# The last tile's mean from TensorE, and 640 columns of the third tile finished by ScalarE and GpSimd, in a role adapter with layernorm

## What is computed

```python
h = jnp.einsum('bsh,bhk->bsk', hidden_states, W_down[role]) + b_down[role][:, None, :]
h = jax.nn.gelu(h, approximate=False)
u = jnp.einsum('bsk,bkh->bsh', h, W_up[role]) + b_up[role][:, None, :]
y = hidden_states + u
mean = jnp.mean(y, axis=-1, keepdims=True)
var = jnp.mean(jnp.square(y - mean), axis=-1, keepdims=True)
yn = (y - mean) * jax.lax.rsqrt(var + LN_EPS)
return yn * gamma[role][:, None, :] + beta[role][:, None, :]
```

## Time and profile before

| | |
|---|---|
| median of 3 runs | 362.35 us (362.21 to 362.82) |
| profiled execution | 362.48 us |
| its span, first to last instruction | 360.7 us |
| TensorE busy | 353.2 us, 98% |
| VectorE busy | 285.6 us, 79% |
| ScalarE busy | 185.0 us, 51% |
| GpSimd busy | 59.8 us, 17% |
| DMA moved | 96.61 MB, mean 268 GB/s |
| granted TensorE clock, mean | 0.998 |

### The profile page before, as it was taken

How to read it: one execution, slowest core, us unless ns; L and a number is a source line. 1 busy time by engine, 2 the same in 40 slices (tenths; PEclk the granted TensorE clock), 3 DMA queues, 4 the chain that set the end, 5 groups by cost and what they waited for, 6 DMA issues and landing times.

```text
span 360.7 us, 4991 instructions
## 1 busy us (share of the span) xinstructions
PE 353.2 (98%) x1559; PEld 290.2 (80%) x1559; DVE 285.6 (79%) x301; ACT 185.0 (51%) x303; POOL 59.8 (17%) x75
## 2 busy tenths in 40 slices
PE   9999999999999999999999999999999999999992
PEld 4888888888888888888888888888888888888882
DVE  3788999298993989759996699957989489893886
ACT  4785556761368415682256814476234862255133
POOL 0000222003220213102140022300232003320003
PEclk9999999999999999999999999999999999999999
DMA  6999999962999549994699927999099981745023
GB/s 187 393 408 409 410 393 358 355 237 87 333 336 362 219 121 370 330 344 172 172 363 343 353 107 244 341 360 352 40 297 348 377 315 53 240 147 204 1 115 120
DMA packets 27804, 96.61 MB, mean 268 GB/s; under 512 B 3218, under 2 KB 3858, under 8 KB 27794
## 3 DMA queue, kind: packets, MB, share of 16 engines
q1 hardware_dynamic: 23186, 81.14, 62.8%
q10 hardware_dynamic: 4608, 15.34, 11.0%
HBM read 79.70 MB, written 16.78 MB: 267 GB/s over the span
## 4 chain that ended last, share of the span: by engine, by line
PE 92%; DVE 3%; ACT 2%; issue 1%; POOL 1%; POOLq 0%; DVEq 0%; ACTq 0%
PE down_ps L311 48%; PE up_ps L318 42%; DVE rows L683 1%; PE up_ps L432 1%; DVE rows L688 1%; ACT squares L488 1%; DVE rows L742 0%; POOL rstd L603 0%; DVE up_ps L720 0%; POOLq L44 0%; ACT h_full L478 0%; ACT h_hi L480 0%; ACT neg_mean_scaled L485 0%; POOL var_eps L601 0%; DVE down_ps L705 0%
## 5 line engine op out<-in xcount | busy, mean ns | idle before, releaser
L311 PE MATMUL down_ps<-x_hi,wd_hi 128*128 128x512 f32 x256 | 81.2, 390 | 0.1
L311 PE MATMUL down_ps<-x_lo,wd_hi 128*128 128x512 f32 x256 | 80.9, 389 | 0.0
L311 PE MATMUL down_ps<-x_hi,wd_lo 128*128 128x512 f32 x256 | 80.8, 389 | 0.0
L318 PE MATMUL up_ps<-wu_hi,h_hi 128*128 128x512 f32 x248 | 76.4, 389 | 0.0
L318 PE MATMUL up_ps<-wu_lo,h_hi 128*128 128x512 f32 x248 | 76.4, 389 | 0.0
L318 PE MATMUL up_ps<-wu_hi,h_lo 128*128 128x512 f32 x248 | 76.3, 389 | 0.0
L601 POOL TENSOR_TENSOR var_eps<-var,eps 128x1 f32<-128x1 f32 x31 | 22.7, 733 | 292.0 <-ACT squares L488 292.0
L485 ACT ACTIVATE neg_mean_scaled<-row_sum 128x1 f32<-128x1 f32 x31 | 6.3, 203 | 124.7 <-DVE rows L688 124.7
L676 DVE TENSOR_TENSOR h_lo<-h_full,h_hi 128x512 fp32r<-128x512 f32 x32 | 22.2, 693 | 46.6 <-ACT h_hi L480 46.6
L311 PEld LDWEIGHTS down_ps<-x_hi,wd_hi 128*128 128x128 f32 x256 | 47.9, 188 | 11.1 <-issue 0.9
L311 PEld LDWEIGHTS down_ps<-x_hi,wd_lo 128*128 128x128 f32 x256 | 48.0, 188 | 10.0
(11 more groups left out here) (64 smaller groups left out, 274.2 us busy)
## 6 DMA issues: line engine op xcount, KB each, us to landing
wu_stage<-W_up SPq DMA_DIRECT2D x32, 512.0 KB, 7.0
rows<-x SPq DMA_DIRECT2D x32, 512.0 KB, 7.4
x_stage<-xT SPq DMA_DIRECT2D x30, 512.0 KB, 7.1
wd_stage<-W_down SPq DMA_DIRECT2D x30, 512.0 KB, 8.6
out<-rows ACTq DMA_DIRECT2D x28, 512.0 KB, 4.6
b_up_row<-b_up SPq DMA_DIRECT2D x8, 512.0 KB, 5.1
gamma_row<-gamma SPq DMA_DIRECT2D x8, 512.0 KB, 9.5
beta_row<-beta SPq DMA_DIRECT2D x8, 512.0 KB, 10.3
```

What stands on the lines that cost most here:

```text
L311: return pe.matmul(down_ps[:, kc, :], wd_part[:, n, c * K + kc * P:c * K + (kc + 1) * P], x_part[:, n, c * S:(c + 1) * S], start=start, st ...
L318: mm = pe.matmul(up_ps[:, t % 2, half], h_part[:, kc, t * P:(t + 1) * P], wu_part[:, kc, half], start=(kc == 0 and h_part is h_hi and wu_p ...
```

## The change

Before the last tile's product is there, its mean can be known: the sum of a row of h·W_up is h times the row sums of W_up. In the last batch ScalarE sums the rows of the four parts of `wu_stage` (`sum_wu`, an Identity with an accumulator over 1024 columns, into `wu_sum`), the sums are split into hi and lo like W_up and placed in two further columns of `wu_hi` and `wu_lo`, whose rows become H + 2 wide for all batches (the second further column is zero). The product of the last tile starts with columns 768 to 1023 and these two (258 columns), so the row sum of the projection lies in PSUM after the first part. ScalarE sums the residual (`sum_last_residual`), and `last_mean` puts both together. The parts are then centred on the true mean at once, into `centred` in SBUF (`centre_part`), squared by ScalarE from there (`part_variance`), multiplied by gamma from `centred` into `rows` (`scale_part`), and finished (`finish_piece`); the shift and its three steps on GpSimd are gone.

The third tile is finished by VectorE for columns 0 to 383 only; ScalarE multiplies the other 640 by the inverse deviation (`scale_tile`) and GpSimd adds beta (`finish_tile_columns`). The third tile's store waits for both.

The diff, cut to its core:

```diff
+    THIRD_COLS = 3 * P
...
-        wu_hi = sb("wu_hi", [P, KC, H], F32R)
-        wu_lo = sb("wu_lo", [P, KC, H], F32R)
+        wu_hi = sb("wu_hi", [P, KC, H + 2], F32R)
+        wu_lo = sb("wu_lo", [P, KC, H + 2], F32R)
+        wu_sum = sb("wu_sum", [P, KC, 2], F32)
...
+        LAST_PARTS = (POOL_PIECE,) + PIECES
+        LAST_BANKS = (down_ps[:, 0, 0:POOL_COLS], last_tile[:, PIECES[0]], last_tile[:, PIECES[1]])
+        LAST_MOVING = (slice(H - POOL_COLS, H + 2),) + PIECES
+        LAST_OUT = (down_ps[:, 0, 0:POOL_COLS + 2],) + LAST_BANKS[1:]
+        PROJECTED_SUM = down_ps[:, 0, POOL_COLS:POOL_COLS + 1]
...
+            sp.wait_ge(pool_third_normed, 1)
+            store_last(NT - 2)
...
-                        for part, bank in zip(LAST_PARTS, LAST_BANKS):
+                        pe.wait_ge(wu_sum_split, 1)
+                        for part, bank in zip(LAST_MOVING, LAST_OUT):
...
+            def sum_wu(i):
...
+                act.activation(squares[:, :], wu_stage[:, i, :], ACT.Identity,
+                               accum_out=wu_sum[:, i, 0:1]).then_inc(wu_sum_ready, 1)
+
+            def sum_last_residual():
+                act.wait_ge(biased, NT * B)
+                act.wait_ge(var_ready, NT * (B - 1) + 2)
+                act.activation(squares[:, :], rows[:, NT - 1, :], ACT.Identity,
+                               accum_out=residual_sum[:, :]).then_inc(residual_sum_ready, 1)
+
+            def part_variance(i):
...
+                act.wait_ge(last_part_centred, i + 1)
+                act.activation(squares[:, LAST_PARTS[i]], centred[:, (NT - 1) % 2, LAST_PARTS[i]], ACT.Square,
+                               scale=H ** -0.5, accum_out=part_var[:, i:i + 1]).then_inc(part_var_ready, 1)
+
+            def scale_tile():
+                t = NT - 2
+                act.wait_ge(scaled, NT * B - 1)
+                act.wait_ge(rstd_ready, NT * B - 1)
+                act.mul(centred[:, t % 2, THIRD_POOL], centred[:, t % 2, THIRD_POOL], rstd[:, t:t + 1]).then_inc(act_third_scaled, 1)
...
+            def finish_tile_columns():
+                t = NT - 2
+                pool.wait_ge(beta_landed, 16 * B)
+                pool.wait_ge(act_third_scaled, 1)
+                pool.tensor_tensor(rows[:, t, THIRD_POOL], centred[:, t % 2, THIRD_POOL], beta_row[:, THIRD_POOL],
+                                   ALU.add).then_inc(pool_third_normed, 1)
...
+            def last_mean():
+
                 dve.wait_ge(last_part_ready, 1)
+                dve.wait_ge(residual_sum_ready, 1)
+                dve.tensor_scalar(last_neg_mean[:, :], PROJECTED_SUM, residual_sum[:, :], -1.0 / H,
+                                  ALU.add, ALU.mult).then_inc(last_mean_ready, 1)
+
+            def centre_part(i):
+                dve.wait_ge(last_mean_ready, 1)
                 dve.wait_ge(last_part_ready, i + 1)
+                dve.scalar_tensor_tensor(out=centred[:, (NT - 1) % 2, LAST_PARTS[i]], in0=LAST_BANKS[i],
+                                         scalar=last_neg_mean[:, :], in1=rows[:, NT - 1, LAST_PARTS[i]],
+                                         op0=ALU.add, op1=ALU.add).then_inc(last_part_centred, 1)
+
+            def scale_part(i):
+                dve.wait_ge(last_part_centred, i + 1)
+                dve.tensor_tensor(rows[:, NT - 1, LAST_PARTS[i]], centred[:, (NT - 1) % 2, LAST_PARTS[i]],
+                                  gamma_row[:, LAST_PARTS[i]], ALU.mult).then_inc(last_part_scaled, 1)
+
+            def finish_piece(i):
                 t = NT - 1
                 dve.wait_ge(rstd_ready, NT * B)
+                dve.wait_ge(last_part_scaled, i + 2)
+                dve.scalar_tensor_tensor(out=rows[:, t, PIECES[i]], in0=rows[:, t, PIECES[i]],
+                                         scalar=rstd[:, t:t + 1], in1=beta_row[:, PIECES[i]],
+                                         op0=ALU.mult, op1=ALU.add).then_inc(normed, 1)
```

More of the change, by code:

```diff
@@ L290, in _ @@
             steps(B - 1)
-            for t in range(NT - 1):
+            for t in range(NT - 2):
                 store_last(t)
+            sp.wait_ge(pool_third_normed, 1)
+            store_last(NT - 2)
             def store_piece(piece):
@@ L559, in steps @@
                     round_next_part(b, 3)
+                if last:
+                    sum_wu(0)
+                    sum_wu(1)
                 variance(b, 0)
+                if last:
+                    sum_wu(2)
+                    sum_wu(3)
+                    round_wu_sum()
                 variance(b, 1)
+                if last:
+                    sum_last_residual()
                 if not last:
@@ L592, in _ @@
             steps(B - 1)
-            last_variance()
+            part_variance(0)
+            scale_tile()
+            part_variance(1)
+            part_variance(2)
             scale_last_columns()
@@ L690, in sum_tile @@
                                          accum_out=row_sum[:, t:t + 1]).then_inc(summed, 1)
-            def sum_first_half():
-                t, half = NT - 1, slice(0, BANK)
-                dve.wait_ge(biased, NT * B)
+            def last_mean():
                 dve.wait_ge(last_part_ready, 1)
-                dve.scalar_tensor_tensor(out=last_tile[:, half], in0=last_tile[:, half], scalar=1.0,
-                                         in1=rows[:, t, half], op0=ALU.mult, op1=ALU.add,
-                                         accum_out=part_sums[:, 0:1]).then_inc(last_part_summed, 1)
@@ L741, in finish_tile @@
                 dve.wait_ge(scaled, NT * b + t + 1)
-                dve.scalar_tensor_tensor(out=rows[:, t, :], in0=centred[:, t % 2, :], scalar=rstd[:, t:t + 1],
-                                         in1=beta_row[:, :], op0=ALU.mult, op1=ALU.add).then_inc(normed, 1)
+                dve.scalar_tensor_tensor(out=rows[:, t, cols], in0=centred[:, t % 2, cols], scalar=rstd[:, t:t + 1],
+                                         in1=beta_row[:, cols], op0=ALU.mult, op1=ALU.add).then_inc(normed, 1)
             def first_steps():
@@ L805, in last_steps @@
                     centre_tile(b, t)
+                    if t == 1:
+                        split_wu_sum()
                     finish_tile(b, t)
                 sum_tile(b, NT - 2)
+                last_mean()
+                centre_part(0)
                 centre_tile(b, NT - 2)
[L809 to L813 removed]
+                scale_part(0)
+                finish_tile(b, NT - 2, THIRD_DVE)
+                centre_part(1)
+                scale_part(1)
+                centre_part(2)
+                scale_part(2)
+                finish_piece(0)
+                finish_piece(1)
             split_first_part()
```

114 lines of the change are left out of this document (44 added, 70 removed).

## The result

| | before | after |
|---|---|---|
| median | 362.35 us | 368.72 us (368.36 to 369.02, 5 runs) |
| profiled execution | 362.48 us | 368.83 us |
| its span | 360.7 us | 366.9 us |
| last matmul ends | 354.09 | 359.14 |
| from there to the span's end | 6.57 | 7.76 |

The ratio to before is 1.017 (1.0156 to 1.0185). That it would be slower was right; the time lies 4.8 us above the forecast and 4.4 above its range. The table says where: 5.05 of the 6.2 us come before the last matmul ends, where the prediction had taken 0.01 and bounded the rest by 0.8, and 1.2 behind it, where it had put 1.15 to 1.58.

A forecast was written before the change was run, and what follows sets the result against it. TensorE, 92% of the chain, bounds the kernel, so only the ladder behind its last matmul moves: pieces +1.30, span +1.58 with the end clash; 362.35 + 1.55 = 363.9, own range 363.3 to 364.3, widened to 362.5 to 364.3.

The forecast's parts named there:

- The step that failed: the row pitch of W_up's halves: All eight batches' W_up rows grow by 8 bytes; bounded by zero and 1 ns a matmul, 0.8 in all, taken as zero.
- third rival: W_up's pitch slows TensorE's matmuls by 1 ns each: 0.8 on top, 363.1 or above; chance 0.05.
- the clash at the end: VectorE's last pieces: GpSimd gets in after the first for 0.6, to 359.14; the second ends at about 359.55; span +1.58.
- Tile 2's add and power: GpSimd in the tail: add waits for VectorE's centring until 352.04, power ends at 352.74 instead of 352.43; cost 0.31.
- ScalarE's 640 columns: Third tile's scaling by the inverse deviation, from 352.80, needing 0.81.
- The disputed price: VectorE's scaling of part 1, two SBUF inputs, waits from 354.16 for GpSimd's 640-column add until 355.22: 1.06.
- The first rival: Tail: VectorE never waits for GpSimd, so +0.13 to +0.45, 362.5 to 362.8; chance 0.25.
- the row at 37.52: x_lo's subtraction on VectorE, started 0.16 into GpSimd's one-column power, took 1.23; the nearest row bounding the wait by nothing.
- rstd: Last tile's inverse deviation, GpSimd's power ending at 357.74; VectorE's pieces follow at 357.79 against 356.49, +1.30.
- the second clash: GpSimd holding up VectorE's second last piece; were it nothing, the last issue would be at 359.15 and the sum +1.15.
- What was to cost nothing: Work ahead of the third tile's sum: W_up's sums, split and residual's sum fit idle time; TensorE's wait has over 1.4 spare.
- The second rival: Tail: no port matters; pieces start at 356.41, last issue at 357.77, −0.23, 362.1; chance 0.07.

The follow-up runs named there:

- e2_shift: The kernel before with an unused 96-byte tensor ahead of `h_full`, moving h and all behind it, W_up's halves as before; 368.59 us (before: 362.49).
- e7_gamma_psum: The changed kernel with gamma copied by ScalarE into two free PSUM banks, where the last tile's three scalings read it; 368.06 us in one run.
- e8_own_columns: The changed kernel with W_up's old rows; the last 256 columns and two sums get own tensors, allocated last; 363.99 us, ratio 1.0032.
- e17_after_pitch256: The changed kernel with W_up's rows 256 bytes longer than before and 224 unused bytes behind `wu_sum`; 363.58 us, ratio 1.0034.
- e9_own_gamma_beta: The changed kernel with old W_up rows, own tensors for the last columns and sums, and tail gamma and last pieces' beta in PSUM; 362.55 us, ratio 1.0000.
- e4_shift_wu_h: The kernel before with 96 unused bytes ahead of `wu_hi`, so W_up's halves and h move together; 363.15 us (before: 362.72).

## Why the prediction was right and wrong

**The step that failed: the row pitch of W_up's halves.** The prediction saw that the rows grow for all eight batches, had no row for it, and bounded it by 0 to 1 ns a matmul, 0.8 in all, with 0 taken "since the means of all such groups are alike whatever they read". It measured 6.4 ns a matmul and 5.0 us. The argument was empty: all groups of the kernel before share one layout, in which every distance between a streamed and a loaded operand is a multiple of 512 bytes, so their equal means say nothing of another. The upper end of 1 ns came from no row either. And the step looked at the pitch alone. The change also moves h by 96 bytes, which by itself costs all of it (`e2_shift`); the prediction's third rival had the right sign and place and was six times too small, with a chance of 0.05. That the kernel came out slower, as forecast, holds for the tail's part alone; most of the 6.4 us has a cause that the forecast put at nothing.

**The tail: the wait was right, the clash at the end was not.** Set against the end of the last matmul, 5.05 later than in the forecast:

- Tile 2's add and power wait for VectorE: forecast 0.43 for the add and its power ending at 352.74; measured 0.52, and 357.64, which is 352.59.
- ScalarE's 640 columns: forecast 0.81, measured 0.83. GpSimd's: 1.52 from the line through two rows, measured 1.54.
- The disputed price, VectorE's wait of 1.06 for GpSimd: forecast near 1.7 for the scaling, measured 1.75, and gone with gamma in PSUM. The first rival, in which VectorE never waits, is refuted, and with it the row at 37.52 as a guide: a power of one column isn't a 640-column add.
- rstd: forecast 357.74, measured 362.70, which is 357.65; VectorE's pieces start 1.19 later than before, where 1.30 was forecast.
- The clash at the end was the wrong way round. Forecast: GpSimd gets in between VectorE's two pieces, needs 0.6, and holds up the second piece. Measured: VectorE's two pieces take 1.15, as in the earlier trace rows, 1.13; it is GpSimd's add that is stretched by 0.30, to 1.02, and it ends at 364.46 − 5.05 = 359.41, later than the 359.14 forecast for it. The last issue, 359.45 in these terms, lies between the two forecast, 359.15 and 359.58. Its store lands in 1.95 instead of 2.2. It is issued 0.57 behind the store ahead of it, where the two lie 0.33 apart before; the three variants with this tail's last add (`e7_gamma_psum`, `e8_own_columns`, `e17_after_pitch256`) have the same 0.57 and 1.95, and why isn't shown.
- Sum: +1.19 in the profile, +1.2 by the ratios of `e8_own_columns` and `e17_after_pitch256`, where 1.58 was taken (1.55 in the last line of the sum) and 1.15 was named for the case without the second clash. That it lies so near to 1.15 is luck: the last issue comes 1.45 later, and the store's quicker landing takes 0.25 of it away.

**What was to cost nothing.** The sums of W_up's rows ran at 338.09 to 340.42 and 346.13 to 348.47, the split at 351.19 for 0.16, while VectorE waited for rstd until 352.13, and the wait of TensorE for it (tile 3 begins at 353.33) never held. The residual's sum ran from 351.23 to 352.3, about half a microsecond earlier than forecast once TensorE's delay is taken off, and long before the square at 355.10. This confirms the forecast that ScalarE's idle time covers them.

**The second rival**, that no port matters, was to give −0.23. It was built as `e9_own_gamma_beta`, and gave 0.0 with an interval of about 0.3 either way. VectorE's pieces start at 356.41, exactly where that rival put them, but by luck: TensorE's last matmul ended at 354.00 in that execution, 0.09 earlier than before. Behind it they start after 2.41, against 2.40 in the kernel before, and GpSimd's last add ends after 3.85, against 3.86. The gain of 0.2 that the rival named went in small steps: 0.03 ahead of the last part's centring, 0.05 from there to the pieces, 0.10 from the pieces to GpSimd's last add (0.71 instead of 0.61). So the idea itself shows no gain here, since the ladder behind the last matmul keeps its length.

Still open is why a distance off by 64, 96 or 128 bytes slows TensorE; nothing between these and 256, and nothing under 64 alone, was tried. That it is the loading of the next weights beside the stream that collides is what the slow matmuls behind each change of product in `e4_shift_wu_h` speak for, but no run shows it by itself. The runs show which distances are slow, not what waits inside.

## What to carry to other kernels

A wider row or a new small tensor moves everything allocated behind it: where TensorE sets the time, keep row lengths and the distances between the operands of a matmul as they were, modulo 256 bytes (as far as tried here), or put the new tensor last, and look at the mean of every matmul group first. A bound for something that no row shows must not be taken from rows that all share the same state. Where GpSimd works in the tail, count VectorE's instructions with two SBUF inputs beside it, and put one of them into PSUM before deciding that an engine is too slow.

## What the runs showed of the hardware that was not expected

- A float32r matmul of 512 columns takes 227 ns from start to start and 232 to 234 when the distance between streamed and loaded operand differs by 64, 96 or 128 bytes from the kernel's; by 256, 512 or 2048 it takes 227. It holds for both products, and 96 bytes that nothing reads cost 6.1 us (1.7%).
- A slow distance outlasts its own pair: in `e4_shift_wu_h` ten matmuls behind each change of product take 2.32 us instead of 2.27, then the pace of before is back.
- Matmuls of 256 columns keep their 0.12 us in either layout (the last tile alone has them: of twelve in a row, the last starts 1.31 behind the first in both kernels).
- VectorE's wait for GpSimd didn't end with GpSimd's instruction alone: the scaling that waited ended 0.55 after it, so most of its own 0.69 came behind. At 362.73, in two back-to-back pieces of VectorE's with GpSimd's add starting at 363.44, it was GpSimd that was held, and VectorE's second piece followed without a gap.
